# Experts: the first product computed transposed, with the weights stationary

## The reference

```python
xf = layernorm(x)                                # [1024, 256]
order = jnp.argsort(flat_idx)                    # 2 experts per token: 2048 pairs, sorted by expert
tok = order // top_k
xs = xf[tok]
h = jax.nn.gelu(jax.lax.ragged_dot(xs, w1, tokens_per_expert), approximate=False)   # w1: 8 x 256 x 1024
ys = jax.lax.ragged_dot(h, w2, tokens_per_expert)                                   # w2: 8 x 1024 x 256
ys = ys * flat_w[order][:, None]
out = jnp.zeros_like(xf).at[tok].add(ys)
```

## Time and profile before

| what | us |
|---|---|
| median of three runs | 3130.3 |
| lowest and highest run | 3129.72, 3131.92 |
| span of the profiled execution, first to last instruction | 3124.2 |
| TensorE busy in it | 2797.3 (90%) |
| VectorE, GpSimd, ScalarE busy | 2640.9, 2190.1, 1875.0 |
| mean granted clock of TensorE | 0.985 of full |

### The profile page before, as it was taken

The page is one execution under the profiler, slowest core; times in us unless marked ns, Lnnn a source line. Parts: engine busy times, 40 slices in busy tenths (PEclk is TensorE's granted clock), DMA queues, the critical chain, the costliest instruction groups (busy, mean ns, idle before and its releaser), DMA issues.

```text
span 3124.2 us, 101333 instructions
## 1 busy us (share of the span) xinstructions
PE 2797.3 (90%) x33450; PEld 2225.3 (71%) x33450; DVE 2640.9 (85%) x6703; ACT 1875.0 (60%) x3733; POOL 2190.1 (70%) x3924
## 2 busy tenths in 40 slices
PE   4889896788888888869899999999999999999997
PEld 2444444666666666647688888888888888888886
DVE  6887886888888888875699999998989988999986
ACT  2666765777777777775455545555545555555553
POOL 3892001666667666645488888888888888888887
PEclk9999998999999999989999999999999999999999
DMA  5987666232223222623444444444444344444441
GB/s 153 361 332 289 244 243 227 73 86 79 73 78 83 80 74 77 224 82 81 96 104 111 107 101 95 104 104 95 101 91 97 94 103 104 96 98 93 108 94 43
DMA packets 367621, 388.79 MB, mean 124 GB/s; under 512 B 118432, under 2 KB 341264, under 8 KB 362320
## 3 DMA queue, kind: packets, MB, share of 16 engines
q1 hardware_dynamic: 346960, 335.42, 38.9%
q0 software_dynamic: 7328, 23.40, 2.4%
q10 hardware_dynamic: 12960, 25.23, 2.2%
HBM read 235.08 MB, written 148.83 MB: 123 GB/s over the span
## 4 chain that ended last, share of the span: by engine, by line
PE 39%; DVE 6%; issue 3%; POOL 2%; ACT 2%; DVEq 0%; POOLq 0%; ACTq 0%
PE banks L150 11%; PE banks L152 11%; PE banks L151 10%; PE banks L1310 2%; PE banks L1295 2%; DVE a_probT_lo L1397 1%; PE banks L1342 1%; ACT a_qT_hi L1199 1%; DVE a_pick L1522 1%; DVE a_y L1541 1%; DVE a_rsum L1409 1%; PE banks L1365 1%; DVE a_wsel L1531 0%; PE banks L1357 0%; ACT a_ynT_hi L1199 0%
## 5 line engine op out<-in xcount | busy, mean ns | idle before, releaser
L1199 ACT ACTIVATE a_qT_hi<-banks 128x512 f16<-128x512 f32 x252 | 150.5, 597 | 700.8 <-PE banks L152 700.8
L383 POOL TENSOR_TENSOR a_probT_lo<-a_expT,a_probT_hi 128x512 f16<-128x512 f32 (+1 forms) x384 | 372.0, 998 | 243.7 <-ACT a_probT_hi L458 243.7
L449 ACT ACTIVATE a_expT<-banks,a_top,w_score_scale 128x512 f32<-128x512 f32 (+1 forms) x384 | 272.2, 709 | 111.4 <-PE banks L544 111.2
L1112 POOL TENSOR_TENSOR a_pn<-a_prob,a_rsum 128x1024 f32<-128x1024 f32 (+1 forms) x256 | 307.2, 1221 | 5.8 <-DVE a_rsum L1411 5.3
L150 PE MATMUL banks<-a_xnT_hi,w_q_hi 128*128 128x256 f16 x1024 | 281.6, 275 | 4.7 <-DVE a_xnT_lo L1395 3.0
L150 PE MATMUL banks<-a_vo_front,a_probT_hi 128*128 128x256 f16 x1024 | 278.9, 272 | 2.7 <-DVE a_probT_lo L1397 2.6
L152 PE MATMUL banks<-a_xnT_hi,w_q_lo 128*128 128x256 f16 x1024 | 280.9, 274 | 0.0
L151 PE MATMUL banks<-a_xnT_lo,w_q_hi 128*128 128x256 f16 x1024 | 280.9, 274 | 0.0
L152 PE MATMUL banks<-a_vo_front,a_probT_lo 128*128 128x256 f16 x1024 | 279.0, 273 | 0.0
L151 PE MATMUL banks<-a_vo_front,a_probT_hi 128*128 128x256 f16 x1024 | 279.0, 272 | 0.0
L1397 DVE SCALAR_TENSOR_TENSOR a_probT_lo<-banks,a_probT_hi 128x512 f16<-128x512 f32 (+1 forms) x384 | 212.6, 582 | 35.7 <-ACT a_probT_hi L1199 35.3
(11 more groups left out here) (400 smaller groups left out, 10655.0 us busy)
## 6 DMA issues: line engine op xcount, KB each, us to landing
vo<-kv_vo_out SPq DMA_DIRECT2D x38, 2048.0 KB, 7.6
a_vo_front<-vo SPq DMA_DIRECT2D x128, 512.0 KB
kt<-kv_k_out ACTq DMA_DIRECT2D x9, 2560.0 KB, 15.0
a_k<-kt SPq DMA_DIRECT2D x64, 308.0 KB, 3.5
kv_raw_e<-in_L_ffn_w POOLq DMA_DIRECT2D x16, 1024.0 KB, 9.7
a_x<-in_x SPq DMA_DIRECT2D x64, 256.0 KB
a_y<-in_x SPq DMA_DIRECT2D x64, 256.0 KB, 2.8
x<-a_y SPq DMA_DIRECT2D x64, 256.0 KB, 2.2
```

The source lines that it names most:

```text
L383: pool.tensor_tensor(probT[b][1][0:rows, first:end, :], expT[b][0:rows, first:end, :], probT[b][0][0:rows, first:end, :], ALU.subtract).th ...
L449: act.activation(expT[1 - h][0:rows, first:end, :], bank, ACT.Exp, bias=top[0:rows, 0:1], scale=weights["score_scale"][0:rows, 0:1]).then_ ...
L1112: last = pool.tensor_tensor(keys_of(pn[h]), keys_of(prob_of(u, h, 2)), rsum[h][:, :].unsqueeze(2).broadcast_to([P, H, n]), ALU.mult)
L1199: act.activation(out, bank[:, 0:cols].rearrange("p (c s) -> p c s", c=out.shape[1]), ACT.Copy, scale=scale)\
```

## The change

The first product is computed transposed. A block of weights of 128 x 128 is stationary and the token rows move, 128 columns, so the hidden values come out as columns of rows: 8 blocks x 2 chunks x 3 = 48 products into the same two banks. Gelu reads them and writes `hid` in the layout that the second product needs. The eight transposes and `tbank` are gone. The copy and the rest (hi and lo) now read `hid` in SBUF. ScalarE does, for each half, gelu and then its own copy, at the start of round j, and the rows, y and weight steps follow. VectorE does `hidden_lo` ahead of `rows_lo`. A new semaphore `hT_read` rises after the first 12 products of `outputs`, and the copy of half 0 of the next slot waits for it. In the last round TensorE waits for gelu before the work of the next layer that uses the same banks.

```diff
@@ -2528,12 +2528,11 @@
     vare, rstd = [sb(f"vare{n}", [P, 1]) for n in range(GATHERS)], [sb(f"rstd{n}", [P, 1]) for n in range(GATHERS)]
     power = sb("power", [P, 1])
     xT = [(sb(f"xT{p}_hi", [P, DC, P], F16), sb(f"xT{p}_lo", [P, DC, P], F16)) for p in range(2)]
-    hid = sb("hid", [P, FF])
+    hid = sb("hid", [P, FC, P])
     hT = sb("hT_hi", [P, FC, P], F16), sb("hT_lo", [P, FC, P], F16)
     y_sb = [sb(f"y{n}", [P, D]) for n in range(Y)]
     xbank = [psum[:, n * BANK:n * BANK + D] for n in range(2)]
-    hbank = psum[:, 2 * BANK:4 * BANK]
-    tbank = [psum[:, (4 + n) * BANK:(5 + n) * BANK] for n in range(2)]
+    hbank = [psum[:, (2 + n) * BANK:(3 + n) * BANK] for n in range(2)]
     ybank = [psum[:, (6 + n) * BANK:6 * BANK + n * BANK + D] for n in range(2)]
 
     power_set, w_in = sem("power_set"), [sem(f"w_in{e}") for e in range(AHEAD, E)]
@@ -2632,21 +2631,13 @@
             pe.wait_ge(w_ready, min(2 * j + 1, 2 * E))
             need(pe, gelu_done, 2 * j)
             for half in range(2):
-                out = hbank[:, half * BANK:(half + 1) * BANK]
-                for c in range(DC):
-                    for n, (x, w) in enumerate(HALVES):
-                        last = nc.tensor.matmul(out, xT[j % 2][x][:, c, :], part(j, w * PART + c * FF + half * BANK, BANK),
-                                                start=c == 0 and n == 0, stop=c == DC - 1 and n == 2)
+                for m in range(FC // 2):
+                    out, at = hbank[half][:, m * P:(m + 1) * P], (half * FC // 2 + m) * P
+                    for c in range(DC):
+                        for n, (x, w) in enumerate(HALVES):
+                            last = nc.tensor.matmul(out, part(j, w * PART + c * FF + at, P), xT[j % 2][x][:, c, :],
+                                                    start=c == 0 and n == 0, stop=c == DC - 1 and n == 2)
                 last.then_inc(h_full, 1)
-
-        def turn_hidden(j):
-            need(pe, hT_ready, 2 * j)
-            for half in range(2):
-                pe.wait_ge(gelu_done, 2 * j + half + 1)
-                for m in range(FC // 2):
-                    at = (half * FC // 2 + m) * P
-                    last = nc.tensor.transpose(tbank[half][:, m * P:(m + 1) * P], hid[:, at:at + P], ident[:, :])
-                last.then_inc(t_full, 1)
 
         def outputs(j):
             pe.wait_ge(w_ready, min(2 * j + 2, 2 * E))
@@ -2657,6 +2648,8 @@
                 for n, (x, w) in enumerate(HALVES):
                     last = nc.tensor.matmul(ybank[j % 2], hT[x][:, m, :], part(j, (2 + w) * PART + m * D, D),
                                             start=m == 0 and n == 0, stop=m == FC - 1 and n == 2)
+                if m == FC // 2 - 1:
+                    last.then_inc(hT_read, 1)
             last.then_inc(y_full, 1)
 
         for j in range(2):
@@ -2665,7 +2658,6 @@
         for j in range(J):
             if j + 2 < J:
                 turn_rows(j + 2)
-            turn_hidden(j)
             if j == J - 2:
                 pe.wait_ge(xT_ready, J - 1)
                 first.tensor_rows()
@@ -2673,6 +2665,7 @@
                 hidden(j + 1)
             else:
                 first.tensor_rows_taken()
+                pe.wait_ge(gelu_done, 2 * J)
                 layer1.tensor_down()
                 layer1.tensor_q()
                 pe.wait_ge(y_ready, J - 1)
@@ -2697,19 +2690,16 @@
                 act.wait_ge(w_ready, 2 * (LAST_RAW[e] + 1))
             act.activation(region(e, n, 0), raw(e, n), ACT.Identity, scale=inverse[:, n, e:e + 1]).then_inc(w_hi, 1)
 
-        def gelu(j):
-            for half in range(2):
-                act.wait_ge(h_full, 2 * j + half + 1)
-                need(act, t_full, 2 * (j - 1) + half + 1)
-                act.activation(hid[:, half * BANK:(half + 1) * BANK], hbank[:, half * BANK:(half + 1) * BANK], ACT.Gelu,
-                               scale=scales[:, 0, j:j + 1]).then_inc(gelu_done, 1)
-
         def hidden_hi(j):
             for half in range(2):
-                act.wait_ge(t_full, 2 * j + half + 1)
-                need(act, y_full, j)
-                act.activation(hT[0][:, half * FC // 2:(half + 1) * FC // 2, :],
-                               tbank[half].rearrange("p (m s) -> p m s", s=P), ACT.Copy, scale=scales[:, 1, j:j + 1])\
+                chunks = slice(half * FC // 2, (half + 1) * FC // 2)
+                act.wait_ge(h_full, 2 * j + half + 1)
+                need(act, hT_ready, 2 * (j - 1) + half + 1)
+                act.activation(hid[:, chunks, :], hbank[half].rearrange("p (m s) -> p m s", s=P), ACT.Gelu,
+                               scale=scales[:, 0, j:j + 1]).then_inc(gelu_done, 1)
+                need(act, *((hT_read, j) if half == 0 else (y_full, j)))
+                act.wait_ge(gelu_done, 2 * j + half + 1)
+                act.activation(hT[0][:, chunks, :], hid[:, chunks, :], ACT.Copy, scale=scales[:, 1, j:j + 1])\
                     .then_inc(hT_hi, 1)
 
         def finish(j):
@@ -2722,17 +2712,14 @@
             rows_hi(j)
         weights_hi(0, 1)
         weights_hi(1, 0)
-        gelu(0)
         for j in range(J):
+            hidden_hi(j)
             if j + 2 < J:
                 rows_hi(j + 2)
-            hidden_hi(j)
             if j > 0:
                 finish(j - 1)
             if j + 1 < E:
                 weights_hi(j + 1, 1)
-            if j + 1 < J:
-                gelu(j + 1)
             if j + 2 < E:
                 weights_hi(j + 2, 0)
             if j == J - 7:
@@ -2781,9 +2768,9 @@
         def hidden_lo(j):
             for half in range(2):
                 dve.wait_ge(hT_hi, 2 * j + half + 1)
-                span = slice(half * FC // 2, (half + 1) * FC // 2)
-                nc.vector.scalar_tensor_tensor(out=hT[1][:, span, :], in0=tbank[half].rearrange("p (m s) -> p m s", s=P),
-                                               scalar=scales[:, 1, j:j + 1], in1=hT[0][:, span, :], op0=ALU.mult,
+                chunks = slice(half * FC // 2, (half + 1) * FC // 2)
+                nc.vector.scalar_tensor_tensor(out=hT[1][:, chunks, :], in0=hid[:, chunks, :],
+                                               scalar=scales[:, 1, j:j + 1], in1=hT[0][:, chunks, :], op0=ALU.mult,
                                                op1=ALU.subtract).then_inc(hT_ready, 1)
 
         for j in range(2):
@@ -2799,9 +2786,9 @@
         weights_lo(0, 1)
         weights_lo(1, 0)
         for j in range(J):
+            hidden_lo(j)
             if j + 2 < J:
                 rows_lo(j + 2)
-            hidden_lo(j)
             if j + 1 < E:
                 weights_lo(j + 1, 1)
             if j + 4 < J:
```

More of the change, by code:

```diff
@@ L2544, in expert_phase @@
     w_hi, w_ready = sem("w_hi"), sem("w_ready")
-    h_full, gelu_done, t_full, hT_hi, hT_ready = (
-        sem("h_full"), sem("gelu_done"), sem("t_full"), sem("hT_hi"), sem("hT_ready"))
+    h_full, gelu_done, hT_hi, hT_ready, hT_read = (
+        sem("h_full"), sem("gelu_done"), sem("hT_hi"), sem("hT_ready"), sem("hT_read"))
     y_full, y_ready, y_stored = sem("y_full"), sem("y_ready"), [sem(f"y_stored{n}") for n in range(Y)]
```

## The result

The changed kernel takes 3144.12 us (median of four runs, 3140.17 to 3146.87), the kernel before on the same occasions 3130.01 us. The ratio is 1.0049, with a 95% interval of 1.0035 to 1.0063: 11 to 20 us slower. The forecast was 3141 us with a range of 3128 to 3151.

What follows compares the result with a forecast made beforehand. TensorE was taken to bound slots 8 to 21, a loop of first products, gelu, weight copy and split slots 1 to 7. +11.0 - 1.2 + .8 = +10.6 on 3124.2 gave 3134.8; plus 6.1, 3141 us (3128 to 3151).

Steps and rivals of the forecast that it cites:

- The step that carried it: First products from slot 8 on: address instructions cost .25 us per group of three, 4.0 us a slot against 2.59.
- Rival A: Slots 8 to 21: address work hides behind the array, first products 2.9 us, time 3124 us; chance .12.
- rival C: From slot 8: address instructions cost .164 us each, first products 5.6 us, +22, 3163 us; chance .05.
- The loop: Slots 8 to 21: first products, 12 second products, copy of half 0, gelu of half 1; 7.13 us a slot, +11.0.
- The three terms: Slots 8 to 21 +11.0 us, slots 1 to 7 -1.2, end of the expert phase +.8; sum +10.6.
- The queue can't run ahead: From slot 8: next first products' address work starts only when gelu has ended, because their bank is single.
- The sign that I gave for the wait: Slots 8 to 21: TensorE idle for .3 to 1.5 us a slot, ended by ScalarE's gelu.
- Slots 1 to 7: ScalarE binds at 7.25 us a slot against 7.85, two slots lose again; slot 8 starts 1.2 us earlier.
- the two waits: Slots 1 to 7: ScalarE's weight copies for experts 4 and 7 wait for a split, about 2.5 us each.
- My sign for rival B: Slots 1 to 7: first products lasting over 3.5 us would show rival B.
- rival B: Slots 1 to 8: weight loads not fully hidden, some 1 us more each, +8, 3149 us; chance .06.
- The end: From slot 22's first products to the next phase's first transposes: 7.0 us against 6.18, +.8.

Runs made afterwards that it cites:

- e1: Changed kernel with the first product's weight addresses fixed in slots 8 to 22 too; ratio .9977 to the kernel before.
- e2: Changed kernel with ScalarE's order gelu, gelu, copy, copy instead of gelu, copy, gelu, copy; 3129.4 us, ratio .9994 to the kernel before.
- e5: Changed kernel with two buffers (four banks) for the first product's banks, so its wait is for the gelu one slot earlier; ratio 1.0005 to the kernel before.
- e10: Changed kernel with dummy products into an unused bank ahead of the first products of slots 2, 4, 5, 6 and 7; ratio 1.0053 to the kernel before.
- e4: Kernel before with the first product's weight addresses fixed; ratio .9990 to the unedited kernel before.
- e9: Changed kernel with two buffers for the first product's banks, paired second products and dummy products ahead of slots 2, 4, 5, 6 and 7; ratio .9984 to the kernel before.
- e3: Changed kernel with both fixed first-product addresses in slots 8 to 22 and ScalarE's order gelu, gelu, copy, copy; ratio .9965 to the kernel before.

## Why the prediction was right, and where not

**The step that carried it held.** The forecast said that from slot 8 on the product's price is set by addresses and not by columns, since the earlier trace rows show .12 us between loads with an address instruction between them and .02 without. Predicted 4.0 us for the first products, measured 3.99 to 4.26; e1 removes just these instructions and gets 2.62. Rival A (the address work hides, 2.9 us) is excluded in the changed kernel, and rival C (.164 each, 5.6 us) too.

**The loop was the right one, but .26 us too short.** 7.39 against 7.13: the first products with the step to the second ones 4.26 (predicted 4.1), 12 second products 1.28 (1.2), the copy .63 (.58). With 14 slots this is the 15.0 in place of 11.0.

**That the time came out within 3 us is partly luck.** The three terms measured +15.0, +1.1 and +1.1, +17.2 in place of +10.6, which on the median of before would be 3147.5. What brings 3147.5 back to 3144 is nothing that the forecast had: the rest of the program, which the change doesn't touch, was 2.9 us shorter in the profiled execution, and the executions of each of the two kernels lie 5 to 7 us apart.

**"The queue can't run ahead" was right and worth more than I gave it.** I named the loop over copy and gelu, but took TensorE's own work as 6.84, a sum in which the address work of the first products never runs under the second products. e2 shows that it does as soon as the queue needn't wait: a slot is 6.67, not the 7.15 that I expected from such a sum. The sign that I gave for the wait, TensorE idle for .3 to 1.5 us a slot, did not come up either: the timeline has .33 us ahead of the first products of slot 12 and at most .05 in the others. The standstill is in the queue, .6 us longer than in e5; on the array the last second products, with their modelled ends, and the transposes cover most of it.

**Slots 1 to 7: right on ScalarE, wrong in the sum, with its sign.** Predicted -1.2, measured +1.1. ScalarE's chain is as forecast: with the clock kept up (e10) its rounds take 7.2 us, the two waits are 2.42 and 2.48 us (predicted 2.5 each), and from the first gelu to the end of the copy for slot 7 it is 48.3 us (1351.27 to 1399.54), where I had 48.1. Two things were missing. One is the clock. The idle stretches of TensorE ahead of the first products of slots 2, 4 and 6 grow from .99, 2.29 and 1.39 us to 1.87, 3.16 and 1.87, and behind them the clock is at .50, in slot 6 from the tenth product on; this costs 1.4 (e10). Before, the first two of these stretches:

```profile
1359.61 0.59 PE L2638 MATMUL banks<-wall,moe_xT_hi 128*128 128x512 f16 x2 [0.99 <-issue]
...
1376.38 0.59 PE L2638 MATMUL banks<-wall,moe_xT_hi 128*128 128x512 f16 x2 [2.29 <-issue]
```

The other is that the transposes of slot 9 stand ahead of the first products of slot 8 in TensorE's queue and wait for their rows:

```profile
1407.90 0.44 PE L2626 MATMUL banks<-ident,moe_xn 128*128 128x128 f32 x2 [0.66 <-DVE moe_xn L2752]
```

The gelu of half 1 of slot 7, which they also wait for, had ended at 1407.26:

```profile
1406.59 0.67 ACT L2698 ACTIVATE moe_hid<-banks,route_scales 128x512 f32<-128x512 f32 x1
```

With the .24 that follow a gelu elsewhere, they would have started at 1407.50 instead of 1408.17, .7 us earlier. The sum is -1.2 + 1.4 + .7 = +.9, against +1.1. My sign for rival B, first products of over 3.5 us in slots 1 to 7, did come up, 4.0 to 4.25 us in slots 2, 4 and 6, but its cause is not rival B: the loads are the same in e10, where the clock stays up and all of them take 2.62, less than my 2.9. The prediction had no term for the clock.

**The end** was right in kind and size: +1.1 against +.8.

The Trainium skill's figure weighed there, 55.6 ns for a product of 128 columns at full clock (page "TensorE: Matmul & The Clock Gate", section "Wait — 56ns, not 53.3ns?"), is what slots at fixed addresses show, 2.62 / 47 = 55.7 ns. The same page's 81 ns for a sustained stream ("Back-to-back issue gap") is not borne out by these 48 in a row.

## What to carry to other kernels

Before exchanging few wide products for many narrow ones, count what each one costs the queue and not only the array: with an address from a register it is .12 us for every new address, free under 512 columns and dear under 128. A wait ahead of such a sequence costs what the queue stands still in it, and not the idleness that the engine's own rows show: here a slot became .7 us shorter without the wait, where the timeline showed .05 us of idleness. A second buffer gave that back, and so did another order on the engine that is waited for. And where a change shortens TensorE's work in a stretch that others bind, it lengthens the idle stretches, and the clock may take the gain: here 1.4 us.

## What the runs showed of the hardware

An address instruction has a record of 46 ns, but takes .12 us of the queue: their starts are .12 apart before, after and with one or two products between them, and two kernels of different kind with 48 of them a slot meet at 6.66 us (e2, e5). The profile's duration of such an instruction is not its price.

Between one level of the granted clock and the other the 128-column products are .107 and .056 us apart in the same slot. The length of TensorE's idle stretch ahead did not decide it: in the changed kernel it was low after 1.87 and 3.16 us; in e1 it stayed up after 2.81 us (slot 4) and was low after 1.87 us (slot 5); in the form of before, 2.29 us of idleness ahead of slot 4 left it at 1.00 in one kernel and brought it to .64 on average in the other (e4). Ahead of slots 2, 4 and 6, where dummy products left at most .38 us of idleness in e10 and e9, it stayed up in both; ahead of slots 5 and 7, where 1.2 to 2.5 us were left, it stayed up in e10 and was low in e9. What else decides is open.

TensorE's busy share is no measure of narrow products: 100% at 5.52 us a slot (e3) and 99% at 7.4.
